# Six local-attention layers on one core: a new order of work on TensorE, ScalarE and VectorE, with the projections seven steps ahead

## The chip, the cores and the metric

The kernel runs on one core of a Trainium2 chip. The metric is the device time of one execution in microseconds (us). Below, a *step* is one pass of the loop over `g`, and *step k* is the step with `g % 8 == k`.

## The reference

One delta-rule layer comes first, then six local-attention layers, each followed by a feed-forward part, over 4 sequences of 1024 tokens with 128 channels, in float32. The change touches only the six layers:

```
def attn_layer(x, Wqkv, qs, ksc, Wo):              # x is shifted by one token in half its channels
    q, k, v = split(x @ Wqkv)                      # 16 heads of 64
    q, k = l2norm(q) * qs, l2norm(k) * ksc
    q = q * cos * scale + rotate_half(q) * sin * scale
    k = k * cos / scale + rotate_half(k) * sin / scale
    out = local_attention(q, k, v)                 # windows of 32, each sees itself and the one before
    return out @ Wo

def ffn_layer(x, g, bln, W1, b1, W2, b2):
    xn = layernorm(x) * g + bln
    a, gate = split(xn @ W1 + b1)
    return a * gelu(gate) @ W2 + b2

for i in range(6):
    x = attn_layer(shift_tokens(x), ...) + x
    x = ffn_layer(shift_tokens(x), ...) + x
```

## The kernel before

`local_layers` cuts each layer into 8 tiles of 128 tokens of all 4 sequences, and each tile into two units `U` of 8 heads. A unit has 12 projections (4 of K, 4 of Q, 4 of V, one for each sequence) and 4 attention steps (two heads each, all sequences). One loop over `g` drives TensorE, ScalarE and VectorE, each with its own order written out by hand; the engines meet only at semaphores. 48 tiles make 384 attention steps, 8 to a tile.

In a step TensorE has these pieces, all in order:
- S, `scores`: two products that write the mask into PSUM (`kmask` by the full identity `idb`, L1112), then 64 small instructions for the scores (L1119). It waits for `sub_done`, VectorE's subtraction of the step before.
- P0, P1, P2, `project` (L1103), the projections of a unit that is used later (`LEAD`). They use two PSUM banks in turn (`a_bank`), and so does every product of the feed-forward part: use n waits until use n-2 has been released (`a_free`). P0 and P1 are released by VectorE's `rotate`, P2 by ScalarE's copy into `v_tok`.
- T0, T1, `turn_heads` (L1133), transposes of normed keys or queries; TP, `turn_probs` (L1140), of the probabilities; TA, `turn_att` (L1169), of the attention's result. All four write one bank, and each waits until ScalarE has copied the one before it (`t_taken`).
- V, `values` (L1158), 64 small instructions; O, `output` (L1181), the output projection.
- `ffn`: one part of the feed-forward part of the tile before, at the end of a step: its mean (L1189), variance (L1192), gates and linear halves (L1208, three products each), and the down projection (L1198).

ScalarE squares P0 and P1 (`square`, L1247), copies what was transposed (`take_heads`, `take_probs`, `take_att`), takes exponents (`exponents`, after `sub_done`) and the norms (`inverse_norms`). VectorE takes the row maximum and subtracts it (`shifted_scores`), multiplies P0 and P1 by the rotation tables (`rotate`, L1400, after ScalarE's square), sums the squares (`sums`), divides the attention's result (`normalise`, after V), copies the last keys of a unit to its front in steps 0 and 4 (`keep_keys`, for which the next keys' `take_heads` waits), and does its own parts of `ffn` and the copies into `xs` (`shifted_in`). GpSimd adds the two rotated halves (`swapped_sum`) and multiplies by the norms; it waits for `rotate` and `inverse_norms`. SyncE moves the values of a unit into `v2` by DMA.

Of the kernel before, what the change touches and what calls it, by code (L numbers as in the profile page):

```python
# [43 lines left out]
FC = 3  # L44
# [5 lines left out]
LN_EXP = "natural_log_exp_and_others"  # L50
LN_SHIFT = 20
# [12 lines left out]
TILES = NT * DEPTH  # L64
# [3 lines left out]
NIT = UNITS * UP  # L68
LEAD = 6
# [831 lines left out]
def ffn_products(g):  # L901
    if g < 8:
        return ()
    return {2: ("mean",), 3: ("var",), 4: tuple(("gate", i) for i in range(FC)),
            5: tuple(("lin", i) for i in range(FC)), 6: ("down",)}.get(g % 8, ())
# [10 lines left out]
def local_layers(nc, sbuf, names, p, banks, y, msk, ident, c, cols, key_mask, rot, weights):  # L916
# [6 lines left out]
    with ExitStack() as ctx:  # L923
# [47 lines left out]
        for g in range(FIRST, LAST):  # L971
            feed, order = g + LEAD < NIT, turns(g)
            for n in range(2):
                if feed:
                    a_use["x", g, n] = len(a_use)
            if feed:
                a_use["x", g, 2] = len(a_use)
            for name in ffn_products(g):
                a_use["c", g // 8 - 1, name] = len(a_use)
            if 0 <= g - 1 < NIT:  # L980
                t_use["att", g - 1] = len(t_use)
            if order:
                t_use[order[0]] = len(t_use)
            if 0 <= g < NIT:
                t_use["p", g] = len(t_use)
            if order:
                t_use[order[1]] = len(t_use)
# [38 lines left out]
        def all_layers():  # L1026
            with nc.Block(no_gpsimd_drain=True) as block:
# [56 lines left out]
                def _(pe):  # L1084
# [126 lines left out]
                    for g in range(FIRST, LAST):  # L1211
                        feed, attend, behind = g + LEAD < NIT, 0 <= g < NIT, 0 <= g - 1 < NIT
                        order = turns(g)
                        if attend:
                            scores(g)
                        if feed:
                            project(g, 0)
                        if behind:
                            turn_att(g - 1)
                        if feed:  # L1220
                            project(g, 1)
                        if order:
                            turn_heads(order[0])
                        if behind:
                            output(g - 1)
# [4 lines left out]
                        if order:  # L1230
                            turn_heads(order[1])
                        if attend:
                            values(g)
# [4 lines left out]
                def _(a):  # L1238
# [60 lines left out]
                    def ffn(t, k):  # L1299
# [14 lines left out]
                        elif k == 4:  # L1314
# [11 lines left out]
                    for g in range(FIRST, LAST):  # L1326
                        feed, attend, behind = g + LEAD < NIT, 0 <= g < NIT, 0 <= g - 1 < NIT
                        order, U = turns(g), (g + LEAD) // 4
                        if feed:
                            square(g, 0)  # L1330
                        if behind:
                            take_att(g - 1)
                        if attend:
                            exponents(g)
                        if feed:
                            square(g, 1)
                        if order:
                            take_heads(order[0])
                        if attend:
                            take_probs(g)  # L1340
                        if feed and g % 2:
                            inverse_norms(2 * U + (g + LEAD) % 4 // 2)
                        if feed:
                            square(g, 2)
                        if order:
                            take_heads(order[1])
# [42 lines left out]
                def _(v):  # L1389
# [76 lines left out]
                    def ffn(t, k):  # L1466
# [25 lines left out]
                        elif k == 5:  # L1492
# [8 lines left out]
                        elif k == 6:  # L1501
# [6 lines left out]
                    for g in range(FIRST, LAST):  # L1508
# [8 lines left out]
                        if 8 <= g and g % 8 == 4:  # L1517
                            ffn(g // 8 - 1, 4)
                        if feed:
                            rotate(g, 1)  # L1520
                        if 8 <= g and g % 8 == 1:
                            ffn(g // 8 - 1, g % 8)
                        if feed:
                            sums(g, 1)
                        if 8 <= g and g % 8 == 0:
                            ffn(g // 8 - 1, 0)
                        if attend:
                            normalise(g)
                        if 8 <= g and g % 8 in (2, 5, 6):
                            ffn(g // 8 - 1, g % 8)  # L1530
                        if g % 8 == 1 and 0 <= g < NIT - 8:
                            shifted_in(g // 8 + 1)
# [131 lines left out]
```

## Time and profile before

| what | value |
|---|---|
| three runs, median (lowest to highest) | 6171.74 us (6170.45 to 6173.91) |
| the profiled execution | 6156.9 us |
| its span, first to last instruction | 6155.0 us |
| first and last score product of the local layers | 2349.2 and 6105.8 us |
| busy over the span: TensorE, its weight loads, VectorE, ScalarE, GpSimd | 86%, 55%, 68%, 45%, 39% |

The local layers are the stretch from about 2350 to 6106 us of the span. Times of engines overlap, so the busy shares do not add up; a wait counts only on the engine that ends last, and an engine's idle time is put down to whatever ended it.

### The profile page before, as it was taken

Reading aid. Unit: us, or ns where it says so; the run is one execution under the profiler, and the core shown is the slowest. Engines: PE = TensorE matmul, PEld = TensorE weight load, DVE = VectorE, ACT = ScalarE, POOL = GpSimd, SP = SyncE. Lnnn points to the kernel's source line nnn. Section 1 sums busy time; section 2 is a strip of 40 time slices with the busy share of each in tenths; the row PEclk is TensorE's granted clock in tenths of the full one; section 3 lists DMA queues with packets and bytes.
Section 4 is the critical chain, followed back from the end, with each engine's and each line's share of the span. In section 5 each row is a group of like instructions: output and inputs, shape, how many; then the busy total and the mean of one; then the engine's idle time right before and its main releaser. Section 6 shows DMA issues by size and latency. Waiting matters only on the chain. (4 is left out here: it accounts for less than half of the span.)

```text
span 6155.0 us, 169853 instructions
## 1 busy us (share of the span) xinstructions
PE 5313.4 (86%) x71376; PEld 3397.7 (55%) x71376; DVE 4157.3 (68%) x6338; ACT 2766.2 (45%) x5037; POOL 2397.5 (39%) x2148
## 2 busy tenths in 40 slices
PE   5878778786868778999999999999999999999997
PEld 3857667585848564444454545554444445545554
DVE  6565665566565647777777777777777777777774
ACT  4232232414132315555555555555555555555554
POOL 2232222222222315444444444444444444444442
PEclk8888888788878879999999999999999999999999
DMA  0000000000000002222222222222222222222222
GB/s 20 3 2 4 1 4 1 4 1 4 1 4 1 3 29 62 55 59 71 64 57 60 66 71 59 60 64 71 60 60 54 74 65 60 60 69 61 57 59 57
DMA packets 255842, 252.15 MB, mean 41 GB/s; under 512 B 29680, under 2 KB 248688, under 8 KB 254704
## 3 DMA queue, kind: packets, MB, share of 16 engines
q1 hardware_dynamic: 255088, 241.29, 15.5%
q8 instruction: 572, 9.37, 0.6%
q14 instruction: 182, 1.49, 0.1%
HBM read 29.90 MB, written 4.19 MB: 6 GB/s over the span
## 5 line engine op out<-in xcount | busy, mean ns | idle before, releaser
L1360 POOL TENSOR_TENSOR turn<-prod 128x512 f32<-128x512 f32 x768 | 984.8, 1282 | 1936.7 <-DVE prod L1400 970.1
L1103 PE MATMUL banks<-w2s,xs 128*128 128x512 f32 x2304 | 1242.7, 622 | 98.4 <-DVE xs L1432 90.5
L1400 DVE TENSOR_TENSOR prod<-banks,tabs 128x1024 f32<-128x1024 f32 x768 | 936.2, 1219 | 113.9 <-ACT sq L1247 113.5
L1247 ACT ACTIVATE sq<-banks 128x512 f32<-128x512 f32 x768 | 459.3, 598 | 954.0 <-PE banks L1103 949.9
L1369 POOL TENSOR_TENSOR turn<-turn,rs 128x512 f32<-128x512 f32 x768 | 833.9, 1107 | 87.9 <-ACT rs L1264 84.1
L660 POOL TENSOR_TENSOR ao<-at,msk 128x512 f32<-128x512 f32 x288 | 388.4, 1360 | 1044.7 <-PE banks L412 563.8
L1133 PEld LDWEIGHTS banks<-msk,turn 128*128 128x128 f32 x3072 | 325.4, 141 | 573.5 <-issue 564.5
L1436 DVE TENSOR_REDUCE mx<-banks 128x8 f32<-128x512 f32 x384 | 265.7, 692 | 378.1 <-PE banks L1119 376.0
L1411 DVE TENSOR_REDUCE ss<-sq 128x8 f32<-128x512 f32 x768 | 519.4, 676 | 1.5
L854 DVE TENSOR_TENSOR tr<-tr,banks 128x512 f32<-128x512 f32 x240 | 165.4, 689 | 510.1 <-PE banks L436 508.8
L614 ACT ACTIVATE p<-banks 128x512 f32<-128x512 f32 x288 | 172.0, 597 | 722.1 <-PE banks L412 722.1
L1133 PE MATMUL banks<-msk,turn 128*128 128x128 f32 x3072 | 482.9, 280 | 3.6 <-ACT ot L1292 1.6
L1103 PEld LDWEIGHTS banks<-w2s,xs 128*128 128x128 f32 x2304 | 352.7, 193 | 151.1 <-DVE xs L1432 99.5
L412 PE MATMUL banks<-tr,ao 128*128 128x128 f32 x2304 | 345.8, 299 | 93.0 <-DVE tt L856 58.0
L1119 PE MATMUL banks<-kx,qt 64*32 64x64 f32 x24576 | 349.8, 224 | 83.0 <-issue 82.7
L1181 PE MATMUL banks<-ot,w2s 128*128 128x512 f32 x768 | 394.9, 596 | 3.8 <-ACT ot L1292 3.8
L412 PEld LDWEIGHTS banks<-tr,ao 128*128 128x128 f32 x2304 | 308.1, 209 | 120.9 <-DVE tt L856 80.9
L1208 PE MATMUL banks<-xf,w2s 128*128 128x512 f32 (+1 forms) x576 | 296.0, 624 | 90.0 <-ACT msk L1321 59.6
L1119 PEld LDWEIGHTS banks<-kx,qt 64*32 64x32 f32 x24576 | 273.1, 105 | 176.0 <-issue 175.8
L1286 ACT ACTIVATE pt<-banks 128x512 f32<-128x512 f32 x384 | 229.3, 597 | 310.9 <-PE banks L1140 310.9
L1446 DVE RECIPROCAL rc<-banks 128x8 f32<-128x8 f32 x384 | 78.7, 205 | 383.0 <-PE banks L1158 382.8
L1158 PE MATMUL banks<-v,pt 64*32 64x66 f32 x24576 | 332.6, 225 | 2.8 <-ACT pt L1286 2.8
(202 smaller groups left out, 9827.0 us busy)
## 6 DMA issues: line engine op xcount, KB each, us to landing
v<-v_tok SPq DMA_DIRECT2D x1152, 132.0 KB
v<-v_tok SPq DMA_DIRECT2D x384, 66.0 KB
v<-v SPq DMA_DIRECT2D x188, 132.0 KB, 2.6
w2s<-in_weights SPq DMA_DIRECT2D x10, 768.0 KB, 4.6
tabs<-in_rot SPq DMA_DIRECT2D x40, 128.0 KB, 2.7
w2s<-in_weights SPq DMA_DIRECT2D x1, 2713.5 KB, 11.0
w2s<-in_weights SPq DMA_DIRECT2D x10, 256.0 KB, 3.0
xin<-in_x SPq DMA_DIRECT2D x8, 256.0 KB, 2.9
```

The costliest lines, as they stand in the source:

```text
L412: last = pe.matmul(p[3 * x][:, b * P:(b + 1) * P], ao[:, 2 * x + i % 2, b, :], tr[:, x, b, :], start=True, stop=True)
L660: g.tensor_tensor(ao[:, 2 * x + i % 2, :, :], at[:, x, :, :], over_batches(msk[:, M_OFF + LEVELS + i, :]), ALU.mult)\
L1103: pe.matmul(a_bank(use), xs[:, t % 2, b * P:(b + 1) * P], w[:, at:at + 512], start=True, stop=True).then_inc(a_done, 1)
L1119: last = pe.matmul(sc[n * WIN:(n + 1) * WIN, h, b * 2 * WIN:(b + 1) * 2 * WIN], qt[r, j, b * P + n * WIN:b * P + (n + 1) * WIN], kx[r, j, ...
L1133: last = pe.transpose(turn_bank[:, i * P:(i + 1) * P], src[:, i * P:(i + 1) * P], ident)
L1158: last = pe.matmul(pv[n * WIN:(n + 1) * WIN, h, b, :], pt[r, g % 2, b * P + n * WIN:b * P + (n + 1) * WIN], v2[r, h2, b, n, i * DV1:(i + 1 ...
L1181: pe.matmul(out_bank, w[:, W_O + j * P:W_O + (j + 1) * P], ot[:, g % 3, :], start=(j == 0), stop=(j == NP2 - 1)).then_inc(o_done, 1)
L1247: a.activation(sq[:, r % 2, :], a_bank(use), ACT.Square).then_inc(sq_done, 1)
L1360: gp.tensor_tensor(turn[:, r % ROTS, :, :].rearrange(halves, s=2), prod[:, r % 2, 0, :, :].rearrange(halves, s=2), prod[:, r % 2, 1, :, :] ...
L1369: gp.tensor_tensor(turn[:, r % ROTS, :, :], turn[:, r % ROTS, :, :], along(rs[:, q % 2, b, :], DH), ALU.mult).then_inc(rot_done, 1)
L1400: v.tensor_tensor(prod[:, r % 2, :, :, :], a_bank(use).rearrange("p (h d) -> p h d", h=HU).unsqueeze(1) .to_broadcast([P, 2, HU, DH]), tab ...
L1411: v.tensor_reduce(ss[:, q % 2, b, :], sq[:, r % 2, :].rearrange("p (h d) -> p h d", h=HU), AX.X, ALU.add).then_inc(red_done, 1)
```

## The change

The attention steps get a new order on three engines, and nothing is computed otherwise:
- `LEAD` grows from 6 to 7.
- TensorE: V of step g moves into step g+1, behind T0, P0, T1 and P1; O moves one step back, to the place behind S; TA moves to the end of the step.
- ScalarE: `take_heads` and `exponents` move ahead of the first `square`; `take_att` and `inverse_norms` move to the end; the table for the gates' Gelu is loaded ahead of `take_probs` in step 5.
- VectorE: `normalise` is now for step g-1, and stands ahead of the second `rotate`; `ffn` parts 0 and 4 stand ahead of `normalise`; `shifted_in` is done in step 7 for the tile after the next.
- Feed-forward part: gates, linear halves and down projection move from steps 4, 5, 6 to 5, 6, 7.

The two mask products with the full identity are in the kernel before too; the diff does not touch them.

```diff
-LEAD = 6
+LEAD = 7
...
-    return {2: ("mean",), 3: ("var",), 4: tuple(("gate", i) for i in range(FC)),
-            5: tuple(("lin", i) for i in range(FC)), 6: ("down",)}.get(g % 8, ())
+    return {2: ("mean",), 3: ("var",), 5: tuple(("gate", i) for i in range(FC)),
+            6: tuple(("lin", i) for i in range(FC)), 7: ("down",)}.get(g % 8, ())
...
                         if attend:
                             scores(g)
+                        if 0 <= g - 2 < NIT:
+                            output(g - 2)
+                        if order:
+                            turn_heads(order[0])
                         if feed:
                             project(g, 0)
-                        if behind:
-                            turn_att(g - 1)
+                        if order:
+                            turn_heads(order[1])
                         if feed:
                             project(g, 1)
-                        if order:
-                            turn_heads(order[0])
                         if behind:
-                            output(g - 1)
+                            values(g - 1)
                         if attend:
                             turn_probs(g)
                         if feed:
                             project(g, 2)
-                        if order:
-                            turn_heads(order[1])
-                        if attend:
-                            values(g)
+                        if behind:
+                            turn_att(g - 1)
...
-                        if feed:
-                            square(g, 0)
-                        if behind:
-                            take_att(g - 1)
+                        if order:
+                            take_heads(order[0])
                         if attend:
                             exponents(g)
                         if feed:
+                            square(g, 0)
+                        if order:
+                            take_heads(order[1])
+                        if feed:
                             square(g, 1)
-                        if order:
-                            take_heads(order[0])
+                        if 8 <= g and g % 8 == 5:
+                            a.preload_act_table_set(GELU)
                         if attend:
                             take_probs(g)
-                        if feed and g % 2:
-                            inverse_norms(2 * U + (g + LEAD) % 4 // 2)
                         if feed:
                             square(g, 2)
-                        if order:
-                            take_heads(order[1])
+                        if behind:
+                            take_att(g - 1)
+                        if feed and (g + LEAD) % 2:
+                            inverse_norms(2 * U + (g + LEAD) % 4 // 2)
...
                         if feed:
                             rotate(g, 0)
                             sums(g, 0)
-                        if 8 <= g and g % 8 == 4:
-                            ffn(g // 8 - 1, 4)
+                        if 8 <= g and g % 8 in (1, 4):
+                            ffn(g // 8 - 1, 0 if g % 8 == 1 else 4)
+                        if 0 <= g - 1 < NIT:
+                            normalise(g - 1)
                         if feed:
                             rotate(g, 1)
-                        if 8 <= g and g % 8 == 1:
+                            sums(g, 1)
+                        if 8 <= g and g % 8 in (1, 2, 6, 7):
                             ffn(g // 8 - 1, g % 8)
-                        if feed:
-                            sums(g, 1)
-                        if 8 <= g and g % 8 == 0:
-                            ffn(g // 8 - 1, 0)
-                        if attend:
-                            normalise(g)
-                        if 8 <= g and g % 8 in (2, 5, 6):
-                            ffn(g // 8 - 1, g % 8)
-                        if g % 8 == 1 and 0 <= g < NIT - 8:
-                            shifted_in(g // 8 + 1)
+                        if g % 8 == 7 and g // 8 + 2 < TILES:
+                            shifted_in(g // 8 + 2)
```

TensorE, step 2 of a tile in the middle of the layers, before (S is L1112 and L1119, P is L1103, TA L1169, T L1133, O L1181, TP L1140, V L1158, the feed-forward mean L1189):

```order
L1112 MATMUL banks<-kmask,idb 128x256 x2
L1119 MATMUL banks<-kx,qt 32x64 x32
L1103 MATMUL banks<-w2s,xs 128x512
L1169 MATMUL banks<-msk,att 128x128 x4
L1103 MATMUL banks<-w2s,xs 128x512
L1133 MATMUL banks<-msk,turn 128x128 x4
L1181 MATMUL banks<-ot,w2s 128x512
L1140 MATMUL banks<-msk,e 128x128 x4
L1103 MATMUL banks<-w2s,xs 128x512
L1133 MATMUL banks<-msk,turn 128x128 x4
L1158 MATMUL banks<-v,pt 32x66 x32
L1189 MATMUL banks<-xf,msk 128x512
```

The same step of the change:

```order
L1112 MATMUL banks<-kmask,idb 128x256 x2
L1119 MATMUL banks<-kx,qt 32x64 x32
L1181 MATMUL banks<-ot,w2s 128x512
L1133 MATMUL banks<-msk,turn 128x128 x4
L1103 MATMUL banks<-w2s,xs 128x512
L1133 MATMUL banks<-msk,turn 128x128 x4
L1103 MATMUL banks<-w2s,xs 128x512
L1158 MATMUL banks<-v,pt 32x66 x32
L1140 MATMUL banks<-msk,e 128x128 x4
L1103 MATMUL banks<-w2s,xs 128x512
L1169 MATMUL banks<-msk,att 128x128 x4
L1189 MATMUL banks<-xf,msk 128x512
```

V no longer stands next to the next S, P0 begins after O and T0, and TA stands last, with the feed-forward product behind it.

VectorE, step 4 of such a tile, before (L1486 and L1490 are `ffn` part 4, L1446 and L1450 `normalise`):

```order
L1436 TENSOR_REDUCE mx<-banks 128x8
L1440 TENSOR_TENSOR e<-banks,mx 128x2x4x64
L1421 COPY kx<-kx 128x16x32
L1400 TENSOR_TENSOR prod<-banks,tabs 128x1024
L1411 TENSOR_REDUCE ss<-sq 128x8
L1486 TENSOR_TENSOR xc<-xc,msk 128x512
L1490 TENSOR_SCALAR xf<-xc,w2s 128x512
L1400 TENSOR_TENSOR prod<-banks,tabs 128x1024
L1411 TENSOR_REDUCE ss<-sq 128x8
L1446 RECIPROCAL rc<-banks 128x8
L1450 TENSOR_TENSOR att<-banks,rc 128x2x4x64
```

The same step of the change, where line numbers are two higher:

```order
L1438 TENSOR_REDUCE mx<-banks 128x8
L1442 TENSOR_TENSOR e<-banks,mx 128x2x4x64
L1423 COPY kx<-kx 128x16x32
L1402 TENSOR_TENSOR prod<-banks,tabs 128x1024
L1413 TENSOR_REDUCE ss<-sq 128x8
L1488 TENSOR_TENSOR xc<-xc,msk 128x512
L1492 TENSOR_SCALAR xf<-xc,w2s 128x512
L1448 RECIPROCAL rc<-banks 128x8
L1452 TENSOR_TENSOR att<-banks,rc 128x2x4x64
L1402 TENSOR_TENSOR prod<-banks,tabs 128x1024
L1413 TENSOR_REDUCE ss<-sq 128x8
```

`normalise` moved ahead of the second `rotate`, and stays behind `ffn` part 4.

ScalarE, the step that holds the gates (L1321), before, which is step 4:

```order
L1247 ACTIVATE sq<-banks 128x512
L1292 ACTIVATE ot<-banks 128x512
L1296 ACTIVATE e<-e 128x512
L1247 ACTIVATE sq<-banks 128x512
L1277 ACTIVATE kx<-banks 128x4x128
L1286 ACTIVATE pt<-banks 128x512
L1253 ACTIVATE v_tok<-banks 128x8x64
L1277 ACTIVATE kx<-banks 128x4x128
L1321 ACT_TABLE_LOAD
L1321 ACTIVATE msk<-banks,w2s 128x512 x2
L1321 ACTIVATE msk<-banks,w2s 85x512
L1323 ACT_TABLE_LOAD
```

And in the change, which is step 5:

```order
L1277 ACTIVATE kx<-banks 128x4x128
L1296 ACTIVATE e<-e 128x512
L1247 ACTIVATE sq<-banks 128x512
L1277 ACTIVATE kx<-banks 128x4x128
L1247 ACTIVATE sq<-banks 128x512
L1340 ACT_TABLE_LOAD
L1286 ACTIVATE pt<-banks 128x512
L1253 ACTIVATE v_tok<-banks 128x8x64
L1292 ACTIVATE ot<-banks 128x512
L1321 ACTIVATE msk<-banks,w2s 128x512 x2
L1321 ACTIVATE msk<-banks,w2s 85x512
L1323 ACT_TABLE_LOAD
```

The table load moved ahead of three copies, and the first square (L1247) moved behind a copy of keys (L1277) and the exponents (L1296).

## Rows read from the trace of the kernel before

**Rows 1.** Windows, local layers: length, busy (instructions) by engine, granted clock, DMA share, GB/s.

```profile
2350.00:6106.00 3756.00, 3494.77 (x59958) 1872.06 (x59956) 2740.98 (x3789) 2041.29 (x3796) 1778.42 (x1514) 0.99 0.25 62
```

**Rows 2.** Waits of TensorE, 2350 to 6106 us: total, times, longest.

```profile
PE banks L1119 <- issue: 82.7, 88, 2.3
PE banks L1103 <- DVE xs L1432: 60.2, 41, 1.9
PE banks L1208 <- ACT msk L1321: 59.2, 47, 1.3
PE banks L1208 <- DVE prod L1400: 27.5, 46, 0.8
PE banks L1112 <- ACT qt L1279: 17.2, 48, 0.5
```

**Rows 3.** Timeline of TensorE, one step 0: start, length, engine, line, operation, idle before.

```profile
4073.49 0.39 PE L1112 MATMUL banks<-kmask,idb 128*128 128x256 bf16 x2 [0.36 <-ACT qt L1279]
...
4074.60 1.13 PE L1103 MATMUL banks<-w2s,xs 128*128 128x512 f32 x2
4075.56 0.60 PE L1169 MATMUL banks<-msk,att 128*128 128x128 f32 x4
4076.00 1.02 PE L1103 MATMUL banks<-w2s,xs 128*128 128x512 f32 x2
...
4080.45 0.86 PE L1158 MATMUL banks<-v,pt 64*32 64x66 f32 x64
4081.25 0.39 PE L1112 MATMUL banks<-kmask,idb 128*128 128x256 bf16 x2
```

**Rows 4.** Timeline of ScalarE in the same step.

```profile
4075.76 0.60 ACT L1247 ACTIVATE sq<-banks 128x512 f32<-128x512 f32 x1 [2.33 <-PE banks L1103]
4076.26 0.59 ACT L1292 ACTIVATE ot<-banks 128x512 f32<-128x512 f32 x1
```

**Rows 5.** Timeline of VectorE in the same step.

```profile
4074.71 0.69 DVE L1436 TENSOR_REDUCE mx<-banks 128x8 f32<-128x512 f32 x1 [0.60 <-PE banks L1119]
4075.43 0.69 DVE L1440 TENSOR_TENSOR e<-banks,mx 128x512 f32<-128x512 f32 x1
4076.04 0.42 DVE L1421 COPY kx<-kx 128x512 f32<-128x512 f32 x1
4076.39 1.23 DVE L1400 TENSOR_TENSOR prod<-banks,tabs 128x1024 f32<-128x1024 f32 x1
4077.53 0.68 DVE L1411 TENSOR_REDUCE ss<-sq 128x8 f32<-128x512 f32 x1
4078.13 1.21 DVE L1400 TENSOR_TENSOR prod<-banks,tabs 128x1024 f32<-128x1024 f32 x1
...
4079.85 0.17 DVE L1462 COPY y<-y 128x4 f32<-128x4 f32 x1
4080.12 0.69 DVE L1472 TENSOR_TENSOR y<-banks,y 128x512 f32<-128x512 f32 x1
4081.35 0.21 DVE L1446 RECIPROCAL rc<-banks 128x8 f32<-128x8 f32 x1 [0.54 <-PE banks L1158]
4081.60 0.69 DVE L1450 TENSOR_TENSOR att<-banks,rc 128x512 f32<-128x512 f32 x1
```

**Rows 6.** Three lines of VectorE's `ffn`: count, shortest/median/longest in ns, first and last start.

```profile
L1478 DVE COPY xf<-y x48: 424/1389/1392, 2431.6 to 6116.1; 64x512 f32<-64x512 f32 x48
...
L1486 DVE TENSOR_TENSOR xc<-xc,msk x48: 683/1392/1407, 2458.6 to 6123.7; 128x512 f32<-128x512 f32 x48
...
L1490 DVE TENSOR_SCALAR xf<-xc,w2s x48: 546/1148/1151, 2460.1 to 6124.5; 128x512 f32<-128x512 f32 x48
```

**Rows 7.** Timeline of VectorE around the end of the down projection.

```profile
4065.52 0.75 DVE L1504 SCALAR_TENSOR_TENSOR y<-banks,w2s,y 128x512 f32<-128x512 f32 x1 [1.84 <-PE banks L1198]
4066.53 0.69 DVE L1436 TENSOR_REDUCE mx<-banks 128x8 f32<-128x512 f32 x1 [0.26 <-PE banks L1119]
```

**Rows 8.** Windows, just after one gap in the scores.

```profile
4013.00:4016.40 3.40, 3.34 (x7) 1.76 (x8) 2.09 (x4) 1.14 (x3) 0.91 (x1) 0.54 0.66 159
```

More of the change, by code:

```diff
@@ L50 @@
 LN_EXP = "natural_log_exp_and_others"
+GELU = "gelu_and_others"
 LN_SHIFT = 20
@@ L979, in local_layers @@
                 a_use["c", g // 8 - 1, name] = len(a_use)
+            if order:
+                t_use[order[0]] = len(t_use)
+                t_use[order[1]] = len(t_use)
+            if 0 <= g < NIT:
+                t_use["p", g] = len(t_use)
             if 0 <= g - 1 < NIT:
                 t_use["att", g - 1] = len(t_use)
-            if order:
-                t_use[order[0]] = len(t_use)
-            if 0 <= g < NIT:
-                t_use["p", g] = len(t_use)
-            if order:
-                t_use[order[1]] = len(t_use)
         def item(g, n):
@@ L1313, in ffn @@
                             a.activation(hid[:, 2, :], hid[:, 1, :], ACT.Exp, scale=-0.5).then_inc(rstd_ready, 1)
-                        elif k == 4:
+                        elif k == 5:
                             if t >= NT and t % NT == 0:
@@ L1335, in _ @@
                         if feed:
+                            square(g, 0)
+                        if order:
+                            take_heads(order[1])
+                        if feed:
                             square(g, 1)
-                        if order:
-                            take_heads(order[0])
+                        if 8 <= g and g % 8 == 5:
+                            a.preload_act_table_set(GELU)
                         if attend:
                             take_probs(g)
-                        if feed and g % 2:
-                            inverse_norms(2 * U + (g + LEAD) % 4 // 2)
                         if feed:
                             square(g, 2)
-                        if order:
-                            take_heads(order[1])
+                        if behind:
+                            take_att(g - 1)
+                        if feed and (g + LEAD) % 2:
+                            inverse_norms(2 * U + (g + LEAD) % 4 // 2)
                         if 8 <= g:
@@ L1491, in ffn @@
                                 .then_inc(xn_ready, 1)
-                        elif k == 5:
+                        elif k == 6:
                             for i in range(FC):
@@ L1500, in ffn @@
                                     .then_inc(a_free[n % 2], 1)
-                        elif k == 6:
+                        elif k == 7:
                             n = a_use["c", t, "down"]
```

## The prediction

> **What bounds the kernel now.** I read the busy time of each engine over the local layers first, then TensorE's waits there, then one step's timeline engine by engine. In the 3756 us of the local layers TensorE is busy for 3494.8 and idle for 261; VectorE, the next, is busy for 2741 [rows 1]. So TensorE's own order sets the time, and the change can only win back idle time, 261 us at most. The list of waits says where that lies: 82.7 us are gaps inside the scores that no engine ends ("issue"), 60.2 are waits for the copy into `xs`, 59.2 for the Gelu of the first gate (whose table is loaded only when the gate is there), 27.5 for VectorE's second rotation, which holds the first gate's bank, and 17.2 for the last queries [rows 2]; that is 246.8 together, and 14 are in small items. The granted clock averages .99, so about 38 us (estimate: .01 of 3756) go to stretches at half clock [rows 1].
>
> **What goes.** All five waits lose their cause. `xs` is copied two steps ahead of its use instead of right before it, the table is loaded while ScalarE would wait, the last queries are turned a step earlier in the order, and the wait for the rotation I count anew below. The 82.7 us of gaps need an argument. They stand in the scores, which follow V directly [rows 3]: V and S are 64 weight loads and 64 products each, 256 instructions in 1.9 us, while the rest of a step is some 30 in 5.9 us. I take the gaps for instructions that arrive late. With V and S at least 1.9 us apart they should go; I leave 10 us, with 0 and 82.7 as bounds. Gone: 236.8.
>
> The Trainium skill's page "Runtime: NRT & Kernel Launch", section "Instruction fetch mechanics", speaks against that: the sequencer fetches blocks of 256 instructions by itself while it runs the block before, and crossing into a new one is mostly hidden. By that the gaps are no matter of supply, and another order of the same instructions leaves all 82.7. Rival 2 below is this case.
>
> **What comes.** I walk one step of the new order with the times of a step that now has no wait inside: S takes 1.11 from its mask to the next product, a product .96, V .80, and four products and four transposes share the rest of 7.76, so .50 a transpose [rows 3]. With the mask at 0: O 1.11, T0 2.07, P0 2.57, T1 3.53, P1 4.03, V 4.99, TP 5.79, P2 6.29, TA 7.25, end 7.75. ScalarE starts a copy .70 after its transpose began and a square 1.16 after its product, and takes .50 between starts [rows 3, 4]. So keys at 2.77, exponents 3.27, square 0 at 3.77 (P0 would allow 3.73). VectorE rotates .63 after a square began; then 1.14 to the sums, .60 to the next, .25 from reciprocal to division, .61 to what follows, .69 for a whole division and 1.21 for a whole rotation [rows 4, 5]. So rotation 0 at 4.40, sums 5.54, reciprocal 6.14, division 6.39 to 7.08, second rotation 7.00 to 8.21. TA at 7.25 just finds its input. But P0 begins 1.46 later than now, and the second rotation has moved behind a division, so the bank of P1 comes free at 8.21, .46 after the step's end. Whenever a feed-forward product stands there, TensorE waits; with a few hundredths to the engine, .5 us. That is so in steps 3, 5, 6 and 7. Where an attention step follows directly, P0's bank is needed only 2.57 later and nothing waits. The other steps:
>
> - Step 1: carry and residual come ahead of the division, .27 and .61 [rows 5]. Division ends at 7.96, TA waits .75.
> - Step 2: after step 1's rotation and sums the two copies of `xf` start at 9.62 on VectorE; the first takes .42, the second .42 to 1.39 [rows 6]. I take .8, so VectorE comes free at 10.85, while the next scores are ready at 9.72 (TA's wait, then 1.22 from mask to maximum [rows 3, 5]). 1.13 late: exponents start at 3.80 instead of 3.27, square 0 and all behind it .53 later, TA waits .4, the rotation ends at 8.74, and the mean starts 1.03 late. Bounds .65 and 1.63 for the two lengths of the copy.
> - Step 4: `keep_keys` ends at 2.97, and the keys' copy on ScalarE waits for it, so all behind it is .23 later. Then `ffn` part 4 stands ahead of the division. Its two operations take .68 or 1.39, and .55 or 1.15 [rows 6]. Now they are covered: the division is needed only when the next step is 2 us old. There is no cover left, as TA needs it in the same step. I take one long and one short length, 2.0 with the gaps between: reciprocal 8.37, division to 9.31, TA waits 2.1. Bounds 1.4 and 2.7.
> - Step 0: after the down projection VectorE still has the `xs` copies. Maximum now follows 1.01 after `y` starts, .26 of it idle [rows 7]; with two copies of .42 each between them it comes .5 later (1.5 if one is long). `keep_keys` and so the keys' copy are late, T1 must wait for that copy: .6 us (bounds .1 and 1.6).
>
> Sum for a tile: .6 + .75 + 1.03 + .5 + 2.1 + 3 × .5 = 6.5 us. 46 tiles have both feed-forward and projections: 298 us (bounds 248 and 399).
>
> **The sum.** -236.8 + 298 = +61. The clock: the half-clock stretches now follow gaps such as those in the scores; one stretch of 3.4 us at .54 [rows 8] costs 1.6 us. The new 2.1 us wait in step 4 may bring one; at every second tile that is 37 us for the 38 that go, so 0 (-38 to +34). The run-in gets one step more, the end one less with projections: between 0 and a step's 7.76, I take 3. Everything else is only moved: the number of TensorE's, ScalarE's and VectorE's operations is the same, GpSimd's and SyncE's programs are not touched, and with seven steps of lead a key tile has three steps instead of two between its projection and its turn, so GpSimd and the value DMAs have more time than now. The two mask products change nothing, being there already. So +64 us on the profiled execution of 6156.9, or 6221. The runs shown have their median at 6171.7, 15 above that execution; on their scale **6236 us**.
>
> **Rivals.**
> 1. As above, but both of `ffn` part 4's operations are long and the clock falls in every tile: step 4 waits 2.7, +28, and +34 of clock: 6298 us. For it: the medians are the long ones. Against it: GpSimd, whose work I hold to lengthen them, has only one sum to do there.
> 2. The gaps in the scores stay as they are: +73, 6309 us. For it: nothing in the rows says what ends them. Against it: they stand right behind 128 short instructions and almost nowhere else.
> 3. The other side: VectorE's operations run at their short lengths in steps 2 and 4, so that TensorE waits 5.4 us a tile (248), and with that the clock does not fall at all: +11 and -38, with the run-in -24, so 6148 us. It decides from 5.15 us of new waits a tile downwards (236.8 / 46). For it: the short lengths exist. Against it: they are the minimum of 48, the medians are three times or twice as long.
> 4. Wait is exchanged for wait, 6160 to 6184 us: the second rotation ends .2 earlier than I count in every step, as the walk has no margin at TA.
>
> **How the numbers follow.** Chances: the forecast .46, rival 1 .18, rival 2 .10, rival 3 .16, rival 4 .10. From no change this kernel's measurement can tell about 0.2%, 12 us. The forecast is 64 above, its own range is 6187 to 6339, with every bound taken by half (steps -25 to +50, gaps -5 to +36, clock -19 to +17); some .03 of its chance falls within 12 us, and of rival 3 a little too. So slower .70, same .12, faster .18. The range over all is 6140 to 6350: below it lies no case but a part of rival 3, above it rivals 1 and 2 together or all upper bounds at once (6444).
>
> **What would show it.** In the changed profile: no wait of projections for `xs`, none of L1208 for ScalarE; the gaps in the scores under 20 us; waits of some .5 us of feed-forward products for the second rotation, in steps 3, 5, 6, 7, about 1 us in step 2; TA waiting for the division, some 2.1 us once a tile and .75 once. The prediction is wrong if TensorE's idle time over the local layers does not grow from 261 to about 320 us; if step 4's wait at TA is under 1 us; or if a step without waits is no longer 7.7 us, since .1 us in each of 384 makes 38.

## The result, and the profile after

The changed kernel took 6200.83 us (median of 5 runs, 6196.58 to 6202.16), the kernel before 6170.45 us in the same comparison (5 runs, 6158.62 to 6173.91): a ratio of 1.0053, 95% interval 1.0041 to 1.0064. It is slower, as forecast, by 30 us instead of 64. The profiled execution took 6200.83 us, with a span of 6198.9.

Windows of the changed kernel over the local layers (2350 us to its last scores), with the columns of [rows 1]:

```profile
2350.00:6148.00 3798.00, 3455.25 (x59907) 1869.06 (x59913) 2656.02 (x3786) 2119.40 (x3795) 1729.22 (x1515) 1.00 0.25 61
```

The stretch is 42 us longer than that of [rows 1]. TensorE's idle time grew from 261 to 343 us, by 82, while its busy time fell by 40. TensorE's waits in it, as in [rows 2]:

```profile
PE banks L1169 <- DVE att L1452: 162.2, 140, 1.9
PE banks L1133 <- ACT kx L1277: 57.2, 95, 2.2
PE banks L1169 <- ACT pt L1286: 25.3, 52, 1.3
PE banks L1189 <- DVE prod L1402: 21.8, 46, 0.5
```

None of the five waits of [rows 2] is left but the one for the rotation, which now comes four times a tile: the gaps inside the scores are gone wholly, and so are the waits for `xs`, for the first Gelu and for the last queries. In their place TA (L1169) waits for the division and, in step 5, for ScalarE's copy of the probabilities (25.3 us), T1 (L1133) waits for the keys' copy, and four kinds of feed-forward products for the second rotation (the last row and three more of 21.2 us each, at L1192, L1198 and L1208). One tile of TensorE's timeline: most of its rows with a wait, the masks that open steps 0 to 4, and the first gate of step 5 (L1208):

```profile
4011.61 0.38 PE L1112 MATMUL banks<-kmask,idb 128*128 128x256 bf16 x2
...
4015.98 0.63 PE L1133 MATMUL banks<-msk,turn 128*128 128x128 f32 x4 [0.85 <-ACT kx L1277]
...
4020.09 0.38 PE L1112 MATMUL banks<-kmask,idb 128*128 128x256 bf16 x2
...
4028.78 0.66 PE L1169 MATMUL banks<-msk,att 128*128 128x128 f32 x4 [1.51 <-DVE att L1452]
4029.27 0.38 PE L1112 MATMUL banks<-kmask,idb 128*128 128x256 bf16 x2
...
4037.28 0.66 PE L1169 MATMUL banks<-msk,att 128*128 128x128 f32 x4 [0.31 <-DVE att L1452]
4038.41 1.12 PE L1189 MATMUL banks<-xf,msk 128*128 128x512 f32 x2 [0.48 <-DVE prod L1402]
4039.37 0.38 PE L1112 MATMUL banks<-kmask,idb 128*128 128x256 bf16 x2
...
4047.55 1.13 PE L1192 MATMUL banks<-msk 128*128 128x512 f32 x2 [0.46 <-DVE prod L1402]
4048.51 0.38 PE L1112 MATMUL banks<-kmask,idb 128*128 128x256 bf16 x2
...
4052.33 0.63 PE L1133 MATMUL banks<-msk,turn 128*128 128x128 f32 x4 [0.29 <-ACT kx L1277]
...
4057.82 0.66 PE L1169 MATMUL banks<-msk,att 128*128 128x128 f32 x4 [1.76 <-DVE att L1452]
...
4065.93 0.63 PE L1169 MATMUL banks<-msk,att 128*128 128x128 f32 x4 [0.45 <-ACT pt L1286]
4066.55 1.98 PE L1208 MATMUL banks<-xf,w2s 128*128 128x512 f32 x4
```

Step by step, listed against forecast: step 0 .85 (.6), step 1 1.51 (.75), step 2 .79 (1.03), step 3 .46 (.5), step 4 2.05 (2.1), step 5 .45 and a later gate's .26, at 4068.79 (.5), steps 6 and 7 .46 each (.5; they stand at 4077.90 and, for the tile before, at 4008.93). Sum 7.29 instead of 6.5. The large miss in this list is step 1. VectorE there and in step 2, and GpSimd's operation in step 1:

```profile
4024.48 1.23 DVE L1402 TENSOR_TENSOR prod<-banks,tabs 128x1024 f32<-128x1024 f32 x1 [1.77 <-ACT sq L1247]
...
4026.22 0.87 DVE L1464 COPY y<-y 128x4 f32<-128x4 f32 x1
4027.19 0.69 DVE L1474 TENSOR_TENSOR y<-banks,y 128x512 f32<-128x512 f32 x1
...
4030.36 1.12 DVE L1479 COPY xf<-y 64x512 f32<-64x512 f32 x1
4031.51 0.42 DVE L1480 COPY xf<-y 64x512 f32<-64x512 f32 x1
```

```profile
4025.79 1.27 POOL L1362 TENSOR_TENSOR turn<-prod 128x512 f32<-128x512 f32 x1 [1.70 <-DVE prod L1402]
```

The carry, 4 columns that took .17 us in [rows 5], takes .87 and ends when GpSimd's sum ends. In the new order it stands right behind the first rotation, that is, just when GpSimd has started its sum. The first row shows VectorE idle for 1.77 us ahead of that rotation.

### The profile page after: what moved, and what is told of

Read it like the earlier page. It is cut to its first block and busy times, and to the rows that moved or that the text cites. A ratio compares the mean times of both kernels' runs of the same rounds, so it can differ in the third digit from the quotient of the medians.

```text
span 6198.9 us, 169853 instructions
## 1 busy us (share of the span) xinstructions
PE 5277.5 (85%) x71376; PEld 3397.6 (55%) x71376; DVE 4076.4 (66%) x6338; ACT 2845.0 (46%) x5037; POOL 2348.3 (38%) x2148
## 5 line engine op out<-in xcount | busy, mean ns | idle before, releaser
L1103 PE MATMUL banks<-w2s,xs 128*128 128x512 f32 x2304 | 1190.9, 599 | 38.5 <-DVE xs L1434 30.4
L1371 POOL TENSOR_TENSOR turn<-turn,rs 128x512 f32<-128x512 f32 x768 | 784.9, 1043 | 6.1
L1133 PEld LDWEIGHTS banks<-msk,turn 128*128 128x128 f32 x3072 | 357.4, 142 | 548.7 <-issue 473.2
L1133 PE MATMUL banks<-msk,turn 128*128 128x128 f32 x3072 | 476.6, 278 | 60.2 <-ACT kx L1277 57.9
L1247 ACT ACTIVATE sq<-banks 128x512 f32<-128x512 f32 x768 | 454.9, 592 | 65.8 <-PE banks L1103 65.6
L1181 PE MATMUL banks<-ot,w2s 128*128 128x512 f32 x768 | 441.7, 657 | 0.7 <-ACT ot L1292 0.7
L1277 ACT ACTIVATE kx<-banks 128x512 f32<-128x512 f32 x384 | 229.4, 597 | 454.4 <-DVE kx L1423 320.1
L1158 PEld LDWEIGHTS banks<-v,pt 64*32 64x32 f32 x24576 | 269.2, 105 | 289.1 <-ACT kx L1277 142.4
L1169 PEld LDWEIGHTS banks<-msk,att 128*128 128x128 f32 x1536 | 161.1, 140 | 477.5 <-DVE att L1452 475.9
L1169 PE MATMUL banks<-msk,att 128*128 128x128 f32 x1536 | 245.3, 282 | 187.5 <-DVE att L1452 162.2
L1279 ACT ACTIVATE qt<-banks 128x512 f32<-128x512 f32 x384 | 228.9, 596 | 374.2 <-PE banks L1133 374.2
L1103 PEld LDWEIGHTS banks<-w2s,xs 128*128 128x128 f32 x2304 | 351.7, 193 | 62.5 <-DVE xs L1434 31.9
```

The source lines that it names most:

```text
L1103: pe.matmul(a_bank(use), xs[:, t % 2, b * P:(b + 1) * P], w[:, at:at + 512], start=True, stop=True).then_inc(a_done, 1)
L1133: last = pe.transpose(turn_bank[:, i * P:(i + 1) * P], src[:, i * P:(i + 1) * P], ident)
L1158: last = pe.matmul(pv[n * WIN:(n + 1) * WIN, h, b, :], pt[r, g % 2, b * P + n * WIN:b * P + (n + 1) * WIN], v2[r, h2, b, n, i * DV1:(i + 1 ...
L1169: last = pe.transpose(turn_bank[:, b * P:(b + 1) * P], att[:, g % 2, b, :, :].rearrange("p h n -> p (h n)"), ident)
L1181: pe.matmul(out_bank, w[:, W_O + j * P:W_O + (j + 1) * P], ot[:, g % 3, :], start=(j == 0), stop=(j == NP2 - 1)).then_inc(o_done, 1)
L1247: a.activation(sq[:, r % 2, :], a_bank(use), ACT.Square).then_inc(sq_done, 1)
```

## The experiments

Each is an edit of the changed kernel (6200.8 us) unless said otherwise, and each ratio is to the kernel before, measured alongside.

**1. Feed-forward part 4 off the chain** (`e1_split_part4`).

```diff
+                        elif k == 5:
                             v.wait_ge(xm_done, t + 1)
...
+                        if 8 <= g and g % 8 in (4, 5):
+                            ffn(g // 8 - 1, g % 8)          # 4: the product, 5: scale and shift
                         if feed:
                             rotate(g, 0)
                             sums(g, 0)
-                        if 8 <= g and g % 8 in (1, 4):
-                            ffn(g // 8 - 1, 0 if g % 8 == 1 else 4)
+                        if 8 <= g and g % 8 == 1:
+                            ffn(g // 8 - 1, 0)
```

> The changed kernel, with VectorE's feed-forward part 4 cut in two and moved into the idle time ahead of the first rotation (its product in step 4, its scaling in step 5). Theory A (TensorE waits at the end of a step for VectorE's chain, and part 4 lies on it): the wait of the attention's transpose for the division, 1.76 us in step 4, goes; the 162 us of such waits fall to about 80, and the time to about 6120 us. Theory B (waits are exchanged, the two operations then delay the first rotation instead): over 6180 us, with as much TensorE idle time as in the changed kernel.

6102.15 us, ratio 0.9889 (0.9872 to 0.9907): 99 us less than the changed kernel, for the place of two operations of VectorE. Its waits:

```profile
PE banks L1169 <- DVE att L1452: 79.2, 92, 1.9
PE banks L1133 <- ACT kx L1277: 57.3, 95, 2.2
```

162 fell to 79, all other waits stood: theory A. 15 more of the 99 us are the clock: of the changed kernel's 11 stretches at half clock (1.2 GHz, not 2.4) in the local layers 2 are left, and what they cost fell from 19 us to 3 (length times what the granted clock lacks to 1). Step 4 alone had cost more than three times what the whole change lost.

**2. Most of VectorE's side work ahead of the first rotation** (`e2_vector_gaps`).

```diff
+                        elif k == 5:
                             v.wait_ge(xm_done, t + 1)
...
+                        if g % 4 == 0 and 2 <= U < UNITS:
+                            keep_keys(U)
                         if attend:
                             shifted_scores(g)
-                        if g % 4 == 0 and 2 <= U < UNITS:
-                            keep_keys(U)
+                        if 8 <= g and g % 8 in (1, 2, 4, 5):
+                            ffn(g // 8 - 1, {1: 0, 2: 1, 4: 4, 5: 5}[g % 8])
+                        if g % 8 == 6 and g // 8 + 2 < TILES:
+                            shifted_in(g // 8 + 2)
                         if feed:
                             rotate(g, 0)
                             sums(g, 0)
-                        if 8 <= g and g % 8 in (1, 4):
-                            ffn(g // 8 - 1, 0 if g % 8 == 1 else 4)
...
-                        if 8 <= g and g % 8 in (1, 2, 6, 7):
+                        if 8 <= g and g % 8 in (2, 6, 7):
                             ffn(g // 8 - 1, g % 8)
-                        if g % 8 == 7 and g // 8 + 2 < TILES:
-                            shifted_in(g // 8 + 2)
```

> As the run before, and VectorE's other parts also stand ahead of the first rotation: carry and residual in step 1, the copies of xf in step 2, the copies into xs in step 6; the keys kept for the next unit stand ahead of the row maximum. Theory A: the waits of the attention's transpose for the division fall from 162 to under 15 us, those of the heads' transposes for ScalarE's copy of keys from 57 to under 5; about 5995 us. Theory B: the idle time of 1.7 us is too short while GpSimd works, the first rotation comes late: over 6080 us.

5922.17 us, ratio 0.9598 (0.9583 to 0.9613): 279 us below the changed kernel, 4% below the kernel before. The waits that are left (the second row is one of four like it, of 20.5 to 21.2 us):

```profile
PE banks L1169 <- ACT pt L1286: 25.8, 52, 1.3
PE banks L1198 <- DVE prod L1402: 21.2, 46, 0.5
```

The waits for the division and for the keys' copy, 219 us, are gone. The time fell by 59 us more: TensorE's busy time fell too, by 51 us at an equal number of products, 19 of them because no half-clock stretch is left; experiment 5 shows what else can lie in busy time. VectorE was never short of time: its work had stood on the wrong side of the first rotation, before which it idled.

**3. The first projection ahead of the heads** (`e3_p0_first`).

```diff
+                        if feed:
+                            project(g, 0)
                         if order:
                             turn_heads(order[0])
-                        if feed:
-                            project(g, 0)
+                        if feed:
+                            project(g, 1)
                         if order:
                             turn_heads(order[1])
-                        if feed:
-                            project(g, 1)
...
-                        if order:
-                            take_heads(order[0])
                         if attend:
                             exponents(g)
                         if feed:
                             square(g, 0)
+                        if order:
+                            take_heads(order[0])
+                        if feed:
+                            square(g, 1)
                         if order:
                             take_heads(order[1])
-                        if feed:
-                            square(g, 1)
```

> The changed kernel, with the first projection ahead of the first heads' transpose on TensorE, and its square ahead of the copy on ScalarE. Theory A (all of VectorE's chain hangs on the start of the first projection): the chain comes .5 us earlier, the 85 us of feed-forward products waiting for the second rotation fall under 10, the 162 us of waits for the division to about 110; about 6070 us. Theory B (ScalarE's copies then come late and TensorE's transposes wait for them): over 50 us of new waits of transposes, and a time within 30 us of 6200.

6098.38 us, ratio 0.9884 (0.9868 to 0.9899), 102 less than the changed kernel.

```profile
PE banks L1169 <- DVE att L1452: 86.5, 87, 1.2
PE banks L1133 <- ACT qt L1279: 71.4, 49, 1.5
PE banks L1133 <- ACT kx L1277: 32.2, 49, 2.8
```

Both theories hold in part. The waits for the second rotation all but vanish and those for the division fall to 86.5, more than expected; but 104 us of waits of transposes for ScalarE come, where the changed kernel had 59. So the chain does hang on the start of the first projection, and ScalarE is next behind it.

**4. Values beside the scores again** (`e4_v_beside_s`).

```diff
+                        if behind:
+                            values(g - 1)
                         if attend:
                             scores(g)
-                        if 0 <= g - 2 < NIT:
-                            output(g - 2)
...
-                        if behind:
-                            values(g - 1)
+                        if 0 <= g - 2 < NIT:
+                            output(g - 2)
```

> The changed kernel, with the values directly ahead of the scores of the next step, and the output projection in the place that the values had. Theory A (the gaps inside the scores are instructions that arrive late when 256 short ones follow each other): gaps that nothing ends come back in the scores, 60 to 85 us in all, with some half-clock stretches; 6260 to 6300 us. Theory C (the gaps had another cause, which the new order removed): under 10 us of them, and a time within 25 us of 6200.

6514.42 us, ratio 1.0558 (1.0541 to 1.0575).

```profile
PE banks L1169 <- DVE att L1452: 216.7, 261, 2.2
PE banks L1133 <- ACT kx L1277: 120.4, 95, 2.2
PE banks L1119 <- issue: 104.5, 102, 2.4
```

The gaps are back, 104.5 us of them: theory A on the cause. The time rose by 314 us, far more than they explain. The scores begin .8 us later in the step and push VectorE's and ScalarE's chain back with them (the first two rows are 118 us above those of the changed kernel), and half-clock stretches cost 94 us instead of 19; that I had not counted. What the gaps are can be read from the trace: with all of TensorE's instructions numbered from the program's start, those that only wait for a semaphore too, all 67 gaps of over half a microsecond in the scores of the kernel before stand at one place in every 256 (numbers 193 and 194, from 0), and so do all 88 in this run. The Trainium skill's page "Runtime: NRT & Kernel Launch", section "Instruction fetch mechanics", gives 256 instructions as the block in which the sequencer fetches; that part agrees. That crossing into a new block is mostly hidden does not hold where 256 short instructions follow each other in 1.9 us.

**5. Experiments 2 and 3 together** (`e5_gaps_and_p0`; the edits are those shown).

> Both edits at once: VectorE's feed-forward parts ahead of the first rotation, and the first projection and its square ahead of the heads. Theory A (both waits hang on VectorE's chain from the first projection, and the two cures add up): the 84 us of feed-forward products waiting for the second rotation, which the parts' move left, fall under 5, and the 104 us of waits of heads' transposes, which the earlier projection brought, under 10, as they came from late exponents; about 5840 us. Theory B (ScalarE's copies are the next bound): over 50 us of waits for ScalarE, at least 5890 us.

5911.77 us, ratio 0.9581 (0.9565 to 0.9596): 10 us below experiment 2 where I expected 80. The listed waits fell nearly as theory A says (feed-forward products for the rotation 3.6 us, transposes 10), but the time did not follow, and stayed in the range of theory B. Windows of experiment 2 and of this one:

```profile
2350.00:5869.10 3519.10, 3404.72 (x59947) 1857.29 (x59948) 2609.99 (x3784) 2115.26 (x3796) 1739.39 (x1516) 1.00 0.27 66
```

```profile
2350.00:5860.20 3510.20, 3434.14 (x59953) 1899.51 (x59952) 2664.66 (x3784) 2155.47 (x3798) 1725.26 (x1516) 1.00 0.27 66
```

TensorE's idle time fell by 38 us and its "busy" time rose by 29, at an equal number of products. A step of the timeline shows why:

```profile
4007.53 0.60 PE L1133 MATMUL banks<-msk,turn 128*128 128x128 f32 x4
4007.96 1.02 PE L1103 MATMUL banks<-w2s,xs 128*128 128x512 f32 x2
4009.01 0.63 PE L1133 MATMUL banks<-msk,turn 128*128 128x128 f32 x4
```

```profile
4008.28 0.59 ACT L1277 ACTIVATE kx<-banks 128x512 f32<-128x512 f32 x1
```

The second transpose comes 1.05 after the projection, instead of .94 in experiment 2, and so just after ScalarE's copy of the first one has ended (4008.28 + .59, and the hand-over). It waits a tenth of a microsecond in nearly every step (the median over the layers is 1.05), and the list of waits does not show it, because the projection before it is modelled as busy until then.

**6. The gates' table one copy later** (`e6_late_table`): experiment 5 with `preload_act_table_set(GELU)` behind `take_probs`.

> As the run before, with the table of the gates loaded behind the copy of the probabilities instead of ahead of it. Theory A (the load of 1.28 us holds up that copy once a tile): the 26 us in which the attention's transpose waits for it go, and no wait for the gates comes; about 5815 us. Theory B (the load only moves the wait on to the gates or to the copy of the values): within 8 us of the run before.

5915.13 us, ratio 0.9586 (0.9571 to 0.96): nothing gained. The wait of TA for that copy fell from 24 to 5 us, but TensorE's busy time rose by 12 and the waits of the gates for the second rotation from none to 7. Theory B: the wait only moved on, here to VectorE's rotation, which ends no earlier.

**7. Lead of six in the new order** (`e7_lead_six`): `LEAD = 6`.

> The changed kernel with the lead of the projections back at six. Theory A (the new order turns the heads 1.4 us earlier in a step than before, so GpSimd's norms of the first key or query tiles are late by about .8 us in every second step): waits of the heads' transposes for GpSimd, some 150 us, and about 6350 us. Theory B (GpSimd had time enough): within 20 us of 6200.

6607.76 us, ratio 1.0708 (1.0692 to 1.0724): far slower than both theories.

```profile
PE banks L1169 <- DVE att L1452: 188.0, 141, 2.4
PE banks L1208 <- ACT msk L1321: 185.9, 46, 4.1
...
PE banks L1133 <- POOL turn L1371: 50.0, 52, 2.1
```

GpSimd's lateness is 50 us, a third of what I expected. The largest new wait is another: with an even lead the norms fall into odd steps, and in step 5 behind the Gelu table that was just loaded. ScalarE then loads three tables more in each such step:

```profile
4070.90 1.28 ACT L1259 ACT_TABLE_LOAD   x1
...
4072.54 1.28 ACT L1264 ACT_TABLE_LOAD   x1
...
4074.17 1.28 ACT L1321 ACT_TABLE_LOAD   x1
```

The granted clock averages .95 in that run's local layers, 1.00 in the changed kernel's: half-clock stretches cost 224 us instead of 19, half of the 407 by which the run is slower. The run tells that the new order, with its norms at the end of a step, does not bear a lead of six; other leads were not run, and what the shorter lead costs by itself is not told apart from the tables and the clock.

**8. The kernel before, again** (`e8_before_again`).

> The kernel before, unchanged, for a second profile of it. Theory D (the gaps in the scores and the half-clock stretches after them differ from execution to execution, and the profiled execution of 6156.9 us had few): an execution of about 6170 us shows 90 to 100 us of such gaps instead of 82.7, or more half-clock time, and the other waits within 3 us of those of the first profile. Theory E (the 14 us between the profiled execution and the median come from elsewhere): gaps within 4 us of 82.7.

6172.11 us, ratio 1.0002 (0.9991 to 1.0013). Its profiled execution took 6174.48 us, 18 more than the first profile's, with these waits:

```profile
PE banks L1119 <- issue: 95.4, 96, 2.3
PE banks L1103 <- DVE xs L1432: 60.4, 43, 1.8
PE banks L1208 <- ACT msk L1321: 59.2, 47, 1.3
PE banks L1208 <- DVE prod L1400: 27.0, 46, 0.7
PE banks L1112 <- ACT qt L1279: 19.7, 49, 2.4
```

The gaps are 13 us longer, the other four together 2: theory D. The gaps are most of what differs between these two executions, and the one behind [rows 2] had fewer.

**9. The output projection late** (`e9_output_late`): experiment 2, with `output(g - 2)` between `project(g, 2)` and `turn_att(g - 1)`, and VectorE's part 0 behind step 1's second sums.

> VectorE's parts ahead of the first rotation as in the second experiment, and the output projection moved from behind the scores to the place ahead of the attention's transpose, so that the first projection begins 1 us earlier while the heads' transposes keep the distance in which ScalarE copies them; carry and residual go behind step 1's sums, as their input comes later. Theory A (the waits of feed-forward products hang on the start of the first projection alone): the 84 us of waits for the second rotation fall under 5, transposes wait no longer than in the second experiment (27 us); about 5840 us. Theory B (about 5912 us is TensorE's own time in any such order): at least 5900 us.

5806.31 us, ratio 0.941 (0.9393 to 0.9427): the fastest version, 365 us below the kernel before.

```profile
2350.00:5753.20 3403.20, 3353.03 (x59945) 1890.59 (x59946) 2625.72 (x3784) 2126.19 (x3796) 1729.67 (x1515) 1.00 0.28 69
```

TensorE idles for 50 us there (3403.2 - 3353.0), and its busy time is 52 below experiment 2's. O now stands between P2 and TA, and P2 to O and O to TA take .86 each, where experiment 2 has .96 from O to T0 and .94 from P2 to TA (medians over the layers). At .18 in each of 384 steps this comes to more than the whole fall:

```profile
4023.00 1.02 PE L1103 MATMUL banks<-w2s,xs 128*128 128x512 f32 x2
4023.86 1.02 PE L1181 MATMUL banks<-ot,w2s 128*128 128x512 f32 x2
4024.72 0.60 PE L1169 MATMUL banks<-msk,att 128*128 128x128 f32 x4
```

Theory A holds, and theory B, a floor near 5912, is refuted.

**10. The carry alone** (`e10_carry_early`).

```diff
+                        if 8 <= g and g % 8 == 1:
+                            carry(g // 8 - 1)
                         if feed:
                             rotate(g, 0)
...
-                            carry(t)
                             v.wait_ge(o_done, 8 * t + 8)
```

> The changed kernel, with only the carry of step 1 (a copy of 4 columns) ahead of the first rotation. Theory A (the carry takes .87 instead of .17 us there, as GpSimd's sum begins just before it, and all of it is on the path): the wait of the attention's transpose in step 1 falls from 1.5 to about .6 us, and the time by 30 to 45 us to about 6163. Theory B (the residual then takes the delay over, or the time is lost in step 2): within 10 us of 6200.

6165.27 us, ratio 0.9987 (0.9976 to 0.9998): 36 us less than the changed kernel, by moving a copy of 4 columns. The wait in step 1 falls to .53:

```profile
4012.60 0.66 PE L1169 MATMUL banks<-msk,att 128*128 128x128 f32 x4 [0.53 <-DVE att L1452]
```

Theory A; step 4's wait, 1.77, stays as it was. With that one copy in place the change would have cost nothing.

## Why the prediction was half right

**What goes: right.** All five waits lost their cause. Of the gaps, of which I left 10 us, none stayed, and experiment 4 brought them back; rival 2 is refuted. (My "some 30" other instructions of a step are products alone; counted with weight loads, like the 256, they are some 56 by [rows 1].) In the run-in the first scores came 2.2 us later (2351.4 for 2349.2; I took 3).

**What comes: right in place and mechanism, with two terms too small.** The waits stood in the steps and behind the operations that the walk named; experiments 1 and 2 took away those of step 4 and of the rest of VectorE's parts, experiments 3 and 9 the one at the feed-forward products. In step 5 the list names the copy of the probabilities, which the early table load holds up; but the first gate starts as the second rotation ends (4066.55; the rotation runs from 4065.28 for 1.22), and experiment 6, which took most of the copy's wait away (on top of experiment 5), gained nothing. The sum was 82 us of new idle time, net, against 61. One term failed in size at "carry and residual, .27 and .61": the carry took .87 as GpSimd's sum had begun, which made step 1's wait 1.51 instead of .75, 35 us over 46 tiles; experiment 10 gives 36 for it. I had allowed for GpSimd's hold in steps 2 and 4 and not in step 1. The other is step 2's "the first takes .42": the first copy of `xf` took 1.12 (the median of all 48 as well) and the second .42, where I took .42 and .8. The listed waits, .79, do not show it. From mask to mask step 2 takes 10.10 us and step 3, with one feed-forward product too and .46 of listed wait, 9.14; so step 2 loses some 1.4 (estimate: .46 + 10.10 - 9.14), and part of it lies in what counts as busy.

**Everything else is only moved, and the clock 0: the step that failed.** With these words the sum put TensorE's busy time at nothing; it fell by 40 us, more than the whole change cost. The clock gave 12 of them. By the trace's clock records the granted clock averages .9918 over the local layers before and .9951 after, which costs 31 and 19 us against full speed; I had 38 and 37. Before, TensorE fell to half clock 18 times, each time just behind a gap in the scores or a wait for `xs`, of 1.1 to 2.3 us; after, 11 times, ten of them just behind step 4's wait of 1.76. I had counted on that wait to bring one in every second tile; it did in 10 of 46. The other 28 come from a shorter step: 7.55 from mask to mask where nothing waits (experiment 2, 4039.58 to 4047.13), against 7.76 [rows 3]; I had counted 7.75. The prediction named this as what would upset it. Some of what was saved was waiting too, of the kind that experiment 5 shows. In the step of [rows 3] TP starts 1.03 after O (at 4077.46), just after ScalarE's copy of T0 has ended (4077.73 + .61, and the hand-over), where .94 is the least from a projection to a transpose:

```profile
4078.49 0.63 PE L1140 MATMUL banks<-msk,e 128*128 128x128 f32 x4
```

```profile
4077.73 0.61 ACT L1277 ACTIVATE kx<-banks 128x512 f32<-128x512 f32 x1
```

.2 less in each of 384 steps would be some 80 us (estimate); the busy time fell by less, as waits hide in the same way in the new order, in step 2 above all. How much each step gave and took was not worked out.

**The scale: wrong, and the second reason.** I added the change to the median as if the profiled execution stood 15 us below it (14 in the comparison shown) by something that both kernels have. Experiment 8 points to the gaps in the scores, which the change removes: of the 18 us between the two profiles of the kernel before, 13 are gaps and 3 are half clock. The executions agree: 12 of the kernel before, run beside experiment 10, lie within 34 us, and 10 of experiment 10, which has no such gaps, within 3. The changed kernel's profiled execution is its median. Between profiles the change costs 44 us, between medians 30.

So 82 us of idle time, less 40 of busy time, and 2 us of the ends make 44 between the profiles, and 30 between medians. The rivals: rival 1's clock fall came in 10 tiles of 46 and not in every one, and only one of part 4's operations was long (1.39; the other took .55); rival 3's short lengths came neither in step 4 nor in step 2 (1.12 and .42); rival 4's earlier second rotation did not come either, with waits of .46 for .5. No rival named what happened.

## What to carry to other kernels

When an order is rewritten so that a late result is needed earlier, walk the chain behind the operation that releases it and ask what else stands in that engine's queue between the two: here VectorE had 1.7 us idle in front of its first rotation and its side work behind it, and moving most of that work ahead of the rotation was worth 279 us. A wait that the list shows at one engine may be only the visible part; compare busy time at equal work, or the steps from start to start, before trusting that idle time has gone (experiment 5, and step 2 above). And compare profiles with profiles and medians with medians: what differs between executions may be the very thing that a change removes.

## What the runs showed of the hardware that was not expected

- Where 256 short instructions of TensorE follow each other in 1.9 us, gaps of up to 2.4 us come in the scores: 82.7, 95.4 and 104.5 us in three profiles with values beside scores, none in the changed kernel's, with 3.8 us of other work ahead of the values and 1.9 behind them. They stand at a fixed place in every block of 256.
- TensorE fell to half clock 18 times in the local layers before, each time just behind 1.1 to 2.3 us without work. But such a pause does not always bring it: step 4's wait of 1.76 did in 10 tiles of 46.
- A product of two SBUF operands on VectorE took .68 us where GpSimd stood still and 1.39 where it worked. The carry of 4 columns took .16 with GpSimd idle, and .17, .48 or .87 with it at work (kernel before, experiment 10, changed kernel): each of these times it ends some .03 after the GpSimd instruction that was running when it began, which had .13, .45 or .85 left. The Trainium skill's page "SBUF — State Buffer", section "SBUF: two separate sides", says that the port pair the two engines share is locked for a whole instruction; the carry agrees.
- Table loads of 1.28 us come back three times where ScalarE alternates between the gates and the norms (experiment 7).
